# Sixteen projections over sixteen heads, and a later start for GpSimd's half of the probabilities

## The reference

```
xn = layernorm(x)
q, k, v = xn @ Wq + bq, xn @ Wk + bk, xn @ Wv + bv      # 16 heads of 32
p = softmax(where(causal, q @ k.T / sqrt(32) + slope_h * (key - 511), min))
attn = (p @ v) @ Wo + bo
ffn = (silu(xn @ gate_w.T) * (xn @ up_w.T)) @ down_w.T    # weights: cubic splines of control points
out = x + attn + ffn
```

## Time and profile before

| | us |
|---|---|
| three runs, median (lowest, highest) | 764.75 (762.54, 765.44) |
| the profiled execution: its time | 765.32 |
| its span, first to last instruction | 763.5 |
| mean granted TensorE clock, share of full | 0.964 |
| attention, up to about | 470 |

### The profile page before, as it was taken

One profiled execution on the slowest core, in us unless ns is written; L12 is line 12 of the kernel. 1 busy time (PEld: TensorE's weight loads), 2 busy tenths in 40 slices (PEclk: granted clock), 3 DMA queues, 4 the chain that ended last, 5 costly groups with the idle time before them and its releaser, 6 DMA issues.

```text
span 763.5 us, 13689 instructions
## 1 busy us (share of the span) xinstructions
PE 679.4 (89%) x4884; PEld 545.8 (71%) x4884; DVE 465.3 (61%) x1290; ACT 444.6 (58%) x705; POOL 329.1 (43%) x191
## 2 busy tenths in 40 slices
PE   4878789989699998899898778788699999999997
PEld 3657667777578776788676665576488888888885
DVE  6278867879867879858799787774333223223122
ACT  4388777877667977787878773553243322233321
POOL 1565644555435644454645440221144235235334
PEclk9989999999799999899999899999999999999999
DMA  7887387476765473863855938993638374243001
GB/s 249 150 191 132 42 253 124 66 136 158 111 171 80 56 111 106 170 133 51 195 90 82 381 103 220 337 263 107 169 104 258 114 243 163 87 130 132 28 1 55
DMA packets 53067, 109.75 MB, mean 144 GB/s; under 512 B 6408, under 2 KB 6664, under 8 KB 51464
## 3 DMA queue, kind: packets, MB, share of 16 engines
q1 hardware_dynamic: 51416, 106.46, 57.0%
q10 hardware_dynamic: 1584, 2.43, 1.2%
HBM read 59.32 MB, written 25.17 MB: 111 GB/s over the span
## 4 chain that ended last, share of the span: by engine, by line
PE 42%; POOL 4%; issue 4%; DVE 3%; DMA 2%; ACT 2%; SPq 1%; POOLq 0%; DVEq 0%; ACTq 0%
PE bank L1493 6%; PE bank L1495 6%; PE bank L1494 6%; PE bank L1480 3%; PE bank L1481 3%; POOL resid L1661 3%; PE bank L638 3%; PE bank L583 3%; PE bank L585 2%; PE bank L584 2%; DMA taps<-windows 2%; PE bank L624 2%; POOL in_lo L1653 1%; PE bank L1468 1%; PE bank L655 1%
## 5 line engine op out<-in xcount | busy, mean ns | idle before, releaser
L1160 POOL TENSOR_TENSOR work<-work 128x1280 f16<-128x1280 f32 x64 | 171.1, 2674 | 176.0 <-ACT work L1057 176.0
L1653 POOL TENSOR_TENSOR in_lo<-inner,in_hi 128x512 fp32r<-128x512 f32 x64 | 83.4, 1305 | 203.5 <-ACT in_hi L1560 203.5
L830 DVE CUSTOM_DVE_ANT_0 work<-bank,dist 128x128 f32<-128x128 f32 (+3 forms) x256 | 115.3, 487 | 67.4 <-PE bank L624 48.6
L1049 ACT ACTIVATE work<-work,neg_max 128x128 f32<-128x128 f32 (+3 forms) x256 | 129.9, 561 | 15.5 <-DVE neg_max L830 15.2
L1610 DVE TENSOR_TENSOR inner<-bank,silu 128x512 f32<-128x512 f32 x64 | 44.1, 689 | 136.8 <-ACT silu L1554 136.8
L1560 ACT CAST in_hi<-inner 128x512 fp32r<-128x512 f32 x64 | 39.7, 621 | 135.6 <-PE bank L1495 134.6
L1057 ACT CAST work<-work 128x1280 f16<-128x1280 f32 x64 | 80.6, 1260 | 62.2 <-PE bank L638 61.7
L638 PE MATMUL bank<-ident,work 128*128 128x128 f16 x1280 | 109.1, 231 | 8.6 <-DVE work L839 6.6
L638 PEld LDWEIGHTS bank<-ident,work 128*128 128x128 f16 x1280 | 78.7, 103 | 44.9 <-issue 33.3
L1493 PE MATMUL bank<-w_room,in_hi 128*128 128x512 f32 x256 | 100.6, 393 | 0.7 <-POOL in_lo L1653 0.7
L1494 PE MATMUL bank<-w_room,in_hi 128*128 128x512 f32 x256 | 99.9, 390 | 0.0
(11 more groups left out here) (100 smaller groups left out, 1304.8 us busy)
## 6 DMA issues: line engine op xcount, KB each, us to landing
q_stack<-parts SPq DMA_DIRECT2D x48, 256.0 KB, 5.6
k_stack<-parts SPq DMA_DIRECT2D x48, 256.0 KB, 6.0
z<-xt_scratch SPq DMA_DIRECT2D x128, 88.0 KB
x_in<-x SPq DMA_DIRECT2D x32, 256.0 KB, 4.0
xt_scratch<-xt_room SPq DMA_DIRECT2D x8, 1024.0 KB, 7.1
xt_room<-xt_scratch SPq DMA_DIRECT2D x6, 1024.0 KB, 10.6
factor<-c_basis SPq DMA_DIRECT2D x5, 1024.0 KB, 11.3
taps<-windows SPq DMA_DIRECT2D x5, 1024.0 KB, 11.2
```

The source lines that it names most:

```text
L830: dve.tensor_tensor_reduce(probs[:, s % 2, OFF[i]:OFF[i] + n], score_bank[i % 2][:, 0:n], dist[:, S - n:S], -slope(s), 3.4e38, ALU.add, AL ...
L1049: e = act.activation(tile, tile, ACT.Exp, bias=neg_max[:, s % 2, i:i + 1], scale=-1.0)
L1160: pool.tensor_tensor(probs16[:, s % 2, 1, :], probs[:, s % 2, :], probs16[:, s % 2, 0, :], ALU.subtract).then_inc(lo_ready, 1)
L1653: pool.tensor_tensor(in_lo[k % 2][:, :], inner[:, k % 2, :], in_hi[:, k % 2, :].bitcast(F32), ALU.subtract).then_inc(il_ready, 1)
```

## The change

The units are spread so that each step has one. Steps 11 and 13 had two, 9 and 10 none (they have the x turns), and 12, 14, 15 one each.

| step | 0 | 1 | 2 | 3 | 4 | 5 | 6 | 7 | 8 | 9 | 10 | 11 | 12 | 13 | 14 | 15 |
|---|---|---|---|---|---|---|---|---|---|---|---|---|---|---|---|---|
| before | k1 | q2 | o0 | k2 | o1 | o2 | o3 | q3 | k3 | | | v0 q0 | k0 | v1 q1 | v2 | v3 |
| after | k1 | v3 | o0 | q2 | k2 | o1 | o2 | o3 | q3 | k3 | v0 | q0 | k0 | v1 | q1 | v2 |

In step 10 the unit stands at the end, ahead of the x turns. DVE's x low halves of the turns of step 9 move from the end of step 10 to between its second and third maximum. The statistics of x tile 3 and the aggregation of tiles 2 and 3 move from step 8 to the end of step 9, POOL's inverse deviation of these two from step 9 to step 10. POOL waits for the first maximum of head s before it starts the low half of head s-1. SP takes turns between storing a sum and loading the next x tile, and issues `load_basis` before the last stack, not after the wait for the last k unit. Before the first batch three V units are computed and not four.

```diff
-UNITS = {0: [("k", 1)], 1: [("q", 2)], 2: [("o", 0)], 3: [("k", 2)], 4: [("o", 1)], 5: [("o", 2)], 6: [("o", 3)],
-         7: [("q", 3)], 8: [("k", 3)], 11: [("v", 0), ("q", 0)], 12: [("k", 0)], 13: [("v", 1), ("q", 1)],
-         14: [("v", 2)], 15: [("v", 3)]}
+UNITS = {0: [("k", 1)], 1: [("v", 3)], 2: [("o", 0)], 3: [("q", 2)], 4: [("k", 2)], 5: [("o", 1)], 6: [("o", 2)],
+         7: [("o", 3)], 8: [("q", 3)], 9: [("k", 3)], 10: [("v", 0)], 11: [("q", 0)], 12: [("k", 0)], 13: [("v", 1)],
+         14: [("q", 1)], 15: [("v", 2)]}
-SPLITS = {13: [(0, 0)], 14: [(0, 1)], ...
+SPLITS = {13: [(0, 0)], 15: [(0, 1)], ...
...
-            early, rest = ([], units) if s == 3 else (units[:1], units[1:])
+            early, rest = ([], units) if s in (3, 10) else (units[:1], units[1:])
...
                 bias_and_max(b, s, (0, 1))
             for of, (kind, n) in units:
-                if kind == "v" and n > 0:
+                if kind == "v":
                     v_take(of, n)
...
-            if s == 11:
+            if s in (10, 11):
                 for of, (_, n) in turns:
                     x_low(of, n)
...
             if s == HALF - 1 and b < B - 1:
-                norm_stats(b + 1, (0, 1))
+                tile_stats(b + 1, 0)
+                tile_stats(b + 1, 1)
+                pair_stats(b + 1, (0, 1))
             if carry and s == HALF:
-                norm_stats(b + 1, (2, 3))
-            if carry and s == 11:
-                v_take(b + 1, 0)
+                tile_stats(b + 1, 2)
+            if carry and s == HALF + 1:
+                tile_stats(b + 1, 3)
+                pair_stats(b + 1, (2, 3))
...
             if halved:
+                if s < H:
+                    pool.wait_ge(t_done, 64 * b + 4 * s + 1)
+                    pool.nop(nofuse=True)
                 probs_low(*halved)
...
-            store_sum(b - 1, 1)
-            store_sum(b - 1, 2)
-            room_for_x(b, 0)
-            room_for_x(b, 1)
-            store_sum(b - 1, 3)
-            room_for_x(b, 2)
-            room_for_x(b, 3)
+            for q in range(1, QT):
+                store_sum(b - 1, q)
+                room_for_x(b, q - 1)
+            room_for_x(b, QT - 1)
+        load_basis(sp)
         stack(B - 1, 3)
 
         sp.wait_ge(pj_full, pj_total(("k", KC - 1), B - 1))
-        load_basis(sp)
         load_chunk(sp, 1)
```

More of the change, by code:

```diff
@@ L413 @@
 HALF = H // 2
-UNITS = {0: [("k", 1)], 1: [("q", 2)], 2: [("o", 0)], 3: [("k", 2)], 4: [("o", 1)], 5: [("o", 2)], 6: [("o", 3)],
-         7: [("q", 3)], 8: [("k", 3)], 11: [("v", 0), ("q", 0)], 12: [("k", 0)], 13: [("v", 1), ("q", 1)],
-         14: [("v", 2)], 15: [("v", 3)]}
+UNITS = {0: [("k", 1)], 1: [("v", 3)], 2: [("o", 0)], 3: [("q", 2)], 4: [("k", 2)], 5: [("o", 1)], 6: [("o", 2)],
+         7: [("o", 3)], 8: [("q", 3)], 9: [("k", 3)], 10: [("v", 0)], 11: [("q", 0)], 12: [("k", 0)], 13: [("v", 1)],
+         14: [("q", 1)], 15: [("v", 2)]}
 TURNS = {2: [("c", 3)], 7: [("c", 0)], 9: [("x", 0), ("x", 1)], 10: [("x", 2), ("x", 3)], 11: [("c", 1)],
          15: [("c", 2)]}
-SPLITS = {13: [(0, 0)], 14: [(0, 1)], 1: [(0, 2)], 2: [(0, 3)], 4: [(1, 0)], 5: [(1, 1)], 6: [(1, 2)], 7: [(1, 3)]}
+SPLITS = {13: [(0, 0)], 15: [(0, 1)], 1: [(0, 2)], 2: [(0, 3)], 4: [(1, 0)], 5: [(1, 1)], 6: [(1, 2)], 7: [(1, 3)]}
 def slope(h):
@@ L444 @@
 STACK = 16 * ROLES
-PJ_FIRST = [("x", t) for t in range(QT)] + [("q", 0), ("k", 0)] + [("v", t) for t in range(QT)] + [("q", 1)] + (
+PJ_FIRST = [("x", t) for t in range(QT)] + [("q", 0), ("k", 0)] + [("v", t) for t in range(3)] + [("q", 1)] + (
     steps_keys(range(HALF), before=False))
@@ L455 @@
 MOMENTS = {12: 0, 13: 1, 14: 2}
-PJ_LAST = [("k", 3), ("c", 1), ("m", 0), ("m", 1), ("m", 2), ("c", 2), ("o", 0), ("o", 1), ("c", 3), ("o", 2), ("o", 3)]
-PJ_LAST_ENDS = [("k", 3), ("c", 1), ("m", 0), ("m", 1), ("m", 2), ("c", 2), ("c", 3)] + [("o", t) for t in range(QT)]
-CARRIED = [("k", 3)] + [("c", c) for c in range(1, KC)] + [("o", t) for t in range(QT)] + [
+PJ_LAST = [("q", 3), ("k", 3), ("c", 1), ("m", 0), ("m", 1), ("m", 2), ("c", 2), ("o", 0), ("o", 1), ("c", 3), ("o", 2), ("o", 3)]
+PJ_LAST_ENDS = [("q", 3), ("k", 3), ("c", 1), ("m", 0), ("m", 1), ("m", 2), ("c", 2), ("c", 3)] + [("o", t) for t in range(QT)]
+CARRIED = [("q", 3), ("k", 3)] + [("c", c) for c in range(1, KC)] + [("o", t) for t in range(QT)] + [
     ("m", m) for m in range(3)]
@@ L750, in attention_tensor @@
         project_qk(0, "k", 0)
-        for t in range(QT):
+        for t in range(3):
             project_v(0, t)
@@ L773, in attention_vector, with tile_stats, pair_stats @@
     def attention_vector(dve):
[L774 to L777, removed]
+        def tile_stats(b, t):
+            dve.wait_ge(x_ld[t], 16 * b + 16)
+            dve.bn_stats(stats[:, t, :], x_in[:, t, :]).then_inc(ln_stats, 1)
+        def pair_stats(b, tiles):
             dve.wait_ge(ln_stats, QT * b + tiles[-1] + 1)
@@ L914, in step @@
                 norm_apply(b + 1, 3)
-            for of, (kind, n) in turns if s not in (3, 11) else []:
+            for of, (kind, n) in turns if s not in (3, 10, 11) else []:
                 (x_low if kind == "x" else ctx_low)(of, n)
@@ L944, in attention_vector @@
         dve.memset(minus_half[:], -0.5).then_inc(small_set, 1)
-        norm_stats(0, (0, 1))
-        norm_stats(0, (2, 3))
+        for n in range(2):
+            for t in (2 * n, 2 * n + 1):
+                tile_stats(0, t)
+            pair_stats(0, (2 * n, 2 * n + 1))
         for t in range(QT):
@@ L974, in attention_vector @@
             for s in range(HALF, H):
-                step(b - 1, s, True, s > HALF)
+                step(b - 1, s, True, s > HALF or b > 1)
             for s in range(HALF):
@@ L980, in attention_vector @@
         for s in range(HALF, H + 3):
-            step(B - 1, s, False, False)
+            step(B - 1, s, False, s == HALF)
             if s - 1 in MOMENTS:
@@ L1075, in step @@
                 exponentials(b, s)
+                if s == 2:
+                    v_high(b, 0, 3)
                 probs_high(b, s)
@@ L1085, in step @@
             for half, t in SPLITS.get((s + 1) % H, []) if s < H else []:
-                if s >= HALF - 1 and carry and half == 0:
-                    v_high(b + 1, half, t)
-                elif s < HALF - 1:
+                if s >= HALF - 1 and half == 0:
+                    if carry:
+                        v_high(b + 1, half, t)
+                elif s < HALF - 1 and (half, t) != (0, 3):
                     v_high(b, half, t)
@@ L1164, in step @@
             halved = back(b, s, 1)
-            if carry and s in (8, 9):
-                inverse_std(b + 1, s - 8)
+            if carry and s == 8:
+                inverse_std(b + 1, 0)
+            if carry and s == 10:
+                inverse_std(b + 1, 1)
             if halved:
+                if s < H:
+                    pool.wait_ge(t_done, 64 * b + 4 * s + 1)
+                    pool.nop(nofuse=True)
                 probs_low(*halved)
```

## The result

| | median us (lowest, highest; runs) | against the kernel before of the same job |
|---|---|---|
| before | 763.64 (760.50, 765.44; 4) | |
| changed | 774.33 (770.17, 777.86; 4) | 1.0132 [1.0090, 1.0174] |
| changed, timed again in five rounds | 771.54 (769.84, 774.00; 6), before 761.89 (19) | 1.0105 [1.0076, 1.0135] |

The change makes the kernel 1.0 to 1.3% slower, 10 us. I had said 761.0, 751 to 769. The profiled execution of the changed kernel is the slowest of its four: 777.86 us, span 776.1, granted clock 0.949. A second one took 769.98, span 768.2, clock 0.962, where the kernel before has 0.964.

A forecast was written before the change was run, and what follows sets the result against it. PE, busy 89% of the span, was taken as the bound, with 8.4 us idle a cycle. Cycles -8.1, last batch +2.3 and clock +2.0 sum to -3.8 on 765.32: 761.5, median forecast 761.0 us, range 751 to 769.

The forecast's parts named there:

- the clock: Half clock after PE's long stand in step 11, 1.7 us if it follows; taken as +2.0 for three cycles, bounds 0 and +15.
- -8.1 + 2.3: Spread units in the first three batches' cycles -8.1 us; last batch +2.3, between 0 and +5.
- Step 10: v0 comes in and x low halves delay the maxima: 6.88 becomes 9.3 us, +2.4, ends +1.2 and +3.4.
- Step 11: PE stands 2.4 to 2.5 us as q0 waits for DVE's x low half: 8.84 becomes 8.5, ends -2.8 and +0.3.
- Step 9: k3 comes in while the first maximum and normalized x come 0.9 to 1.1 us earlier: 9.33 becomes 8.2, -1.1.
- Step 13: Loses a unit: 8.45 becomes 5.60 us, -2.85 a cycle, called the surest term.
- Step 8: PE's own work unchanged, k3 becomes q3; idle 0.88 us before the first maximum hangs on step 7: change 0.
- The start: First batch: fourth V unit leaves, nothing won as first scores wait 1.10 us for DMA; k2 in step 4 +0.6.
- The second batch: Steps 9 and 10 go from 19.34 to 17.5 us, -1.85; with steps 11 and 13, -5.0 in all.
- The collision: Second batch, step 9: normalizations took 3.38 us beside POOL's low half instead of 0.99; the new wait prevents this.
- The last batch: k stack misses head 12's first score by 1.8 us, `taps` waits +1.2 more, multiplication -1.1: sum +2.3, between 0 and +5.
- the second, half clock: PE stands in three steps a cycle, paying the low clock in steps 11 and 12: 13.5 instead of 2.0, 772.4 us; chance 0.14.

The follow-up runs named there:

- experiment 7: Changed kernel plus unread matmuls in the first batch, 62 ahead of the first scores and 40 in step 2: 768.23 us, ratio 1.0104.
- experiment 8: Changed kernel with step 10's two x low halves moved behind the first two copies of the turned probabilities: 765.27 us against 763.91, ratio 1.0028.
- all four stands filled: Changed kernel plus unread matmuls in steps 10 and 11, ahead of the first scores and in step 2: 764.19 us against 763.91, ratio 1.0013.
- experiment 3: Changed kernel plus unread matmuls in PE's stands, 26 in step 10 and 30 in step 11: 767.19 us, ratio 1.0051.
- experiment 4: Changed kernel again 771.54 us; with x tile 1 loaded earlier 770.29 (1.0082); with the fourth V unit before the first head 771.13 (1.0102).
- experiment 1: POOL's wait for the first maximum taken out of the changed kernel: 771.28 us (1.0086); added alone to the kernel before: 765.44 against 764.17 (1.0018).
- experiment 5: Changed kernel with v0 back in step 11, x low halves in their old place: 761.00 us (0.9998); plus earlier x tile 1 and fourth V unit: 760.98 (0.9971).
- the best arrangement: Changed kernel with v0 back in step 11, x tile 1 loaded earlier, fourth V unit before the first head: 760.98 us (0.9971); without POOL's wait 759.73 (0.9970).

## Why the prediction was wrong

**The step that failed is the clock.** The prediction put it at "+2.0 for three cycles", one hit of 1.7 us in step 11, softened. Each cycle had up to three hits, in steps 8, 10 and 11, of 1.6 us each, and the start two more stretches at half clock. In the profiled execution these are all three steps in the second and third batch (9.6 us), steps 10 and 11 in the first (3.2), and the start (3.8, from experiment 7; 3.3 against the kernel before): 16.6 us. With my other terms, -8.1 + 2.3, that makes +10.8; the span grew by 12.6. That execution is the slowest of its kind. The second profile, a more usual one, had four hits in the steps, one of them in part, and the start. In the seven profiles that have step 10's stand of 1.9 to 2.3 us, half clock followed in 17 of 21 cycles; behind step 11's of 2.4 us, again in seven profiles, in 11 of 21. At 1.6 us each that is an estimate of 6.4 us for three cycles, beside 3.3 for the start, where I had 2.0 in all. By the medians, filling the stands is worth 0.9 to 1.2% (1.0105 and 1.0132 against 1.0013), 7 to 9 us. I had the rows at hand: steps 9 and 10 of the kernel before had 0.72 and 0.89 behind a stand of 2.30. I reasoned that half clock costs little where PE waits anyway, which was true of the old step 9, but did not go through the new stands asking which has bound work behind it. I had myself predicted one stand of 2.4 us in step 11 and gave half clock 0.14, as the rival that came true. PEclk of 0.83 in step 11 is the sign that the prediction names for it.

**Step 10** I gave 9.3; at full clock it is 9.0, at half clock 10.6. The cause was as supposed, the low halves between the maxima (experiment 8), and they raised PE's stand to 1.93. That such a stand brings the clock down was missing. **Step 11** I gave 8.5 with a stand of "2.4 to 2.5"; it is 8.50 at full clock and the stand is 2.37 on `xt_room`: right, with the clock 10.09. **Step 9** I gave 8.2, it is 7.82. **Step 13** is 5.60, as said. **Step 8** I left at 0, and it is 0 to +1.1 at full clock (6.94 in the third batch of the kernel with all four stands filled, 7.66 in experiment 8, 8.03 in the second batch of experiment 3) and +2.4 here: I looked at DVE's order and not at when the sum of tile 2 is ready, whose store x tile 1's load stands behind; the statistics wait 0.71 for the load, the stand of PE grows from 0.88 to 1.69, and the clock follows.

At nearly full clock (last column of the table) the third batch is -2.2, against my -1.85: there the waits were right. The second is -2.1 against -5.0, of which 3.2 are its step 8 of 10.11; the first is +1.6 against -1.25. Together the four batches are -1.0 where I had -5.8, so some 5 us of the miss are waits priced at nothing or too low, and not the clock of the filled stands. (The bounds "from -15 to -1" for the cycles don't follow from those of the steps either: these give -19 and -3.)

**The start** was the second miss, and steps 0 to 7 of the first batch moved by 5.4 us, which the prediction names as a sign of being wrong. "Nothing is won, since the first scores wait 1.10 us for the DMA" is true and missed the point: the V unit that left the start had covered this DMA, so PE stood 3.82 instead. With full clock this is free (38.31 is the start of the scores in experiment 7, 38.86 before), but half clock follows; in experiment 4 the V unit was back, the stand was 1.16, and half clock came behind stands of 1.99 and 2.16 in steps 1 and 2 instead. Beside it, k2 in step 4 and the sums in step 5 cost 1.45 + 0.84 (first maximum to first maximum, 5.02 to 6.47 and 5.11 to 5.95) where I had estimated 0.6.

**The second batch** should have won 5.0. The collision went as said: the normalization, and GpSimd's low half beside it, in order of time in step 9 of the second batch of the changed kernel (rows of before: the earlier trace rows):

```profile
204.63 2.64 POOL L1169 TENSOR_TENSOR work<-work 128x1280 f16<-128x1280 f32 x1 [4.60 <-DVE neg_max L831]
...
209.04 0.99 DVE L790 TENSOR_SCALAR x_in<-x_in,meanvar,rstd 128x512 f32<-128x512 f32 x2
```

0.99 for the two in place of 3.38, and POOL's 2.64 us, which end at 207.27, lie ahead of them. The normalization is a `tensor_scalar` and not an instruction with two tensors from SBUF, the case that the prediction quotes. The same section of the Trainium skill (SBUF — State Buffer, "Who interferes with whom") also names `tensor_scalar` among the VectorE instructions that can take the port pair shared with GpSimd, and says that whoever issues first has the pair for the whole instruction; the trace agrees, with 2.93 us for one of the two beside POOL's 2.61 and 0.54 apart from it. But three hits of the clock gave 4.8 of the gain back. And without the wait the normalization is as free of POOL (experiment 1), so the wait, my reason for the gain, was not its cause; the new order of the steps was enough.

**The last batch** was about right in sum (+1.0 to +1.7, said +2.3). The stack's wait came, larger, and the wait for the chunk did not:

```profile
439.69 0.76 PE L624 MATMUL bank<-k_stack,q_stack 96*128 96x256 f32 x2 [2.97 <-issue]
...
445.77 0.69 DVE L328 TENSOR_TENSOR taps<-taps,factor 128x512 f32<-128x512 f32 x1 [0.21 <-DMA taps<-windows]
```

2.97 us for the scores of head 12 (said 1.8; the last of the k stack's three DMAs landed at 439.6), but 0.21 for `taps` where it was 2.07 and I had said +1.2; the multiplication went from 1.73 to 0.69, as said. Half clock lay over 10.3 us of steps 11 and 12 here (433.9 to 444.2), beside stands of 1.91 and 2.97, and over 6.8 us of step 13 before.

Of the rivals the second, half clock, gave 772.4: within 2 us of both medians, and at 0.14 the least likely of my list. Its mechanism is what the runs show; that its number fits so well is in part luck, since it rests on the cycles' -8.1, of which the kernel with filled stands shows -2.7.

What stays open: why the same step has half clock in one batch and not in the next. In the second profile PE stood 1.93 us in step 10 of the third batch and the step took 8.89, and 1.91 us in the first batch, where it took 10.45. No run here tells what decides between them, and so none tells why the arrangement of experiment 5 had so few hits in one profile and, without the wait, three in another at the same ratio.

## What to carry to other kernels

A unit moved from a full step into one where its engine waits is not free: cut the kernel at the steps, list where TensorE would stand afterwards (1.7 to 3.8 us here), and charge each such stand with the half clock on the bound work behind it, 1.6 us here in half to four fifths of the cycles, before counting a gain. Leave the engine's waits together in few steps whose work is short; what stands behind them can still be hit, but fewer times. Ask of every unit that moves what its result releases: here the output projection of tile 2 released the load of x. Where a stand can't be moved, useless matmuls in it can pay (0.9 to 1.2% here for four stands), as long as they end before what it waits for.

## What the runs showed of the hardware

Unread matmuls (0.055 us each at 128x112) in stands of 1.9 to 3.8 us raised the mean granted clock of the ten executions of the changed kernel, 0.949 to 0.962, to 0.965 to 0.982 in twelve, and took 7 to 9 us off a kernel whose other work they left as it was. With the stands left, the clock fell to 0.50 behind a stand of 1.69 us (step 8), of 1.93 (step 10) and of 2.37 (step 11), not in every batch. In the best arrangement PE stood 1.75 us in step 10 with 1.00 behind it in each of the three cycles of one profile, and with 0.50 in each of three in the profile of the same arrangement without GpSimd's wait. That wait, which I had argued about at length, changed the time by nothing that 12 runs can tell.
